# Scan runs' beginning: the second half's exponentials, logarithms and du moved behind the first units

## What is computed

```
xdbl = xm @ W_xp
dtr, Bm, Cm = jnp.split(xdbl, [DTR, DTR + DS], axis=-1)      # 64 + 16 + 16
dt = jax.nn.softplus(dtr @ W_dt + b_dt)
A = -jnp.exp(A_log)
def step(hst, inp):                                          # over 1024 positions
    dA = jnp.exp(dt_t[:, :, None] * A)
    hst = hst * dA + (dt_t * x_t)[:, :, None] * B_t[:, None, :]
    y = jnp.einsum('bds,bs->bd', hst, C_t)
```

## Time and profile before

| | |
|---|---|
| median of three executions | 1942.12 us (1942.08 to 1942.58) |
| the profiled execution | 1945.84 us |
| its span from first to last instruction | 1943.5 us |
| busy: TensorE, VectorE, ScalarE, GpSimd | 95%, 82%, 73%, 54% |
| mean granted TensorE clock | 0.975 |
| first scans of runs 0 to 5 | 208.2, 446.3, 669.9, 853.7, 1083.5, 1265.7 us |

### The profile page before, as it was taken

How to read it: one execution, slowest core, us unless ns; L and a number is a source line. 1 busy time by engine, 2 the same in 40 slices (tenths; PEclk the granted TensorE clock), 3 DMA queues, 4 the chain that set the end, 5 groups by cost and what they waited for, 6 DMA issues and landing times.

```text
span 1943.5 us, 32682 instructions
## 1 busy us (share of the span) xinstructions
PE 1845.3 (95%) x12312; PEld 1337.9 (69%) x12312; DVE 1600.7 (82%) x2125; ACT 1425.8 (73%) x2661; POOL 1048.6 (54%) x603
## 2 busy tenths in 40 slices
PE   6989899999999999999999999999998999999997
PEld 3664899948998599969995799689974333332323
DVE  5565899768998699989995999889987999999742
ACT  3426899468993899799974999799954377777775
POOL 3031599526994299939980699479944400003000
PEclk9989899998999999999999999999999799999999
DMA  5023111021111111101110121021101111111000
GB/s 202 1 85 99 59 57 55 32 72 43 56 59 37 51 54 60 51 24 55 56 44 2 40 60 56 24 72 58 58 15 32 38 42 38 37 37 36 17 23 22
DMA packets 57547, 95.18 MB, mean 49 GB/s; under 512 B 14951, under 2 KB 23559, under 8 KB 55982
## 3 DMA queue, kind: packets, MB, share of 16 engines
q1 hardware_dynamic: 55854, 88.90, 15.2%
q0 software_dynamic: 1536, 4.20, 0.7%
HBM read 73.55 MB, written 6.91 MB: 41 GB/s over the span
## 4 chain that ended last, share of the span: by engine, by line
PE 63%; POOL 14%; ACT 8%; DVE 8%; issue 6%; DMA 1%; SPq 1%; DVEq 0%; ACTq 0%; POOLq 0%
POOL A L1019 13%; PE PS L865 10%; PE PS L840 10%; PE PS L256 8%; PE PS L1603 6%; PE PS L1556 6%; PE PS L1763 5%; PE PS L846 5%; PE PS L265 3%; DVE A L1569 2%; PE PS L441 2%; PE PS L872 1%; ACT A L931 1%; ACT A L908 1%; PE PS L243 1%
## 5 line engine op out<-in xcount | busy, mean ns | idle before, releaser
L1019 POOL TENSOR_TENSOR A<-A 128x1024 f32<-128x1024 f32 x384 | 897.6, 2396 | 223.2 <-ACT small L923 111.0
L931 ACT ACTIVATE A<-A,negA 128x512 f32<-128x512 f32 x768 | 547.3, 715 | 34.0 <-DVE A L1000 24.4
L1000 DVE TENSOR_TENSOR_SCAN A<-A,PS 128x512 f32<-128x512 f32 x384 | 436.2, 1201 | 44.8 <-PE PS L846 23.8
L1000 DVE TENSOR_TENSOR_SCAN A<-A,small,PS 128x512 f32<-128x512 f32 x384 | 451.2, 1259 | 5.3 <-ACT A L931 5.3
L865 PE MATMUL PS<-ident,A 128*128 128x128 f32 x3072 | 408.5, 276 | 20.4 <-ACT A L737 13.3
L840 PE MATMUL PS<-A 128*128 128x128 f32 x3072 | 393.8, 276 | 0.9 <-ACT A L915 0.6
L865 PEld LDWEIGHTS PS<-ident,A 128*128 128x128 f32 x3072 | 352.3, 143 | 30.0 <-ACT A L737 15.9
L840 PEld LDWEIGHTS PS<-A 128*128 128x128 f32 x3072 | 368.1, 192 | 2.3 <-DVE A L1000 2.0
L1569 DVE TENSOR_REDUCE A<-PS 128x1 f32<-128x512 f32 x512 | 319.3, 681 | 38.9 <-PE PS L1556 37.3
L1800 ACT ACTIVATE A<-PS 128x512 f32<-128x512 f32 x512 | 267.2, 603 | 101.9 <-PE PS L1763 101.6
L908 ACT ACTIVATE A<-A,small 128x512 f32<-128x512 f32 x320 | 228.6, 714 | 17.3 <-PE PS L846 16.8
(11 more groups left out here) (194 smaller groups left out, 1842.7 us busy)
## 6 DMA issues: line engine op xcount, KB each, us to landing
A<-scrc SPq DMA_DIRECT2D x192, 256.0 KB, 3.1
A<-A SPq DMA_DIRECT2D x360, 32.0 KB
scr<-A SPq DMA_DIRECT2D x4, 1024.0 KB, 4.8
W<-in_wa SPq DMA_DIRECT2D x2, 1536.0 KB, 9.7
X<-in_x SPq DMA_DIRECT2D x4, 512.0 KB, 5.3
scr<-W SPq DMA_DIRECT2D x128, 1.5 KB
out<-X SPq DMA_DIRECT2D x4, 512.0 KB, 2.9
W<-in_w SPq DMA_DIRECT2D x1, 1984.0 KB, 7.3
```

Source lines behind the costliest of these rows:

```text
L931: e.activation(A_B[i % 4], r.DT[:, dt, ci * 512:(ci + 1) * 512], ACT.Exp, scale=negA[:, r.n, dt * 16 + s:dt * 16 + s + 1]).then_inc(*decay ...
L1000: e.tensor_tensor_scan(h, a, u, init, ALU.mult, ALU.add).then_inc(*scanned.up((q, i)))
L1019: e.tensor_tensor(h, h, CB[k % 2].unsqueeze(1).broadcast_to([128, 2, 512]), ALU.mult).then_inc(*weighed.up((q, pair)))
```

## The change

The first half of the sequence goes through its inputs alone. In `inputs_s` the exponentials and logarithms are cut in two (two channel groups d at a time, 1024 columns), and those of the second half move into `run_s`, behind the first diagonals and ahead of `more(3)`; VectorE's delta and du of the second half move into `run_v`, ahead of scan 4; the transposes of its du move in `run_t` behind `form_u(7)`, all four together; only |v| and max(v, 0) of the second half stay. `more(3)` moves on TensorE from behind du's transposes to behind `form_u(3)`. `PARTS` becomes 0, 2, 2, 4, and layer 1's fused product is cut into three: first half at `more(1)`, second at `more(2)`, bias at `more(3)`. VectorE, not ScalarE, copies the second half's x_dbl. ScalarE scales all four du tiles of the first half in every run, and copies two; VectorE copies the other two. `form_u(0)` to `form_u(3)` lie in banks of dt, not of du, and no longer wait for the copies; `form_u(4)` does. What VectorE does `meanwhile` (adding a gathered layer output to X, or X's moments) comes ahead of its first max(v, 0).

```diff
@@ project_dt_t
-            w.wait_ge(*act.at(("xd_twin", r.q, c)))
+            w.wait_ge(*(act if c == r.order[0] else dve).at(("xd_twin", r.q, c)))
@@ inputs_t
             more(1)
-            banks.seek(3)
+            banks.seek(4)
             project_dt_t(e, w, r, r.order[1])
...
             more(2)
-            banks.seek(4)
+            banks.seek(0)
             for j in range(4):
                 turn_du_t(e, w, r, 0, j)
-            more(3)
-            banks.seek(0)
@@ inputs_s
+        def decline_s(e, w, r, p, d):
+            g = DUD[:, p, 2 * d:2 * d + 2, :]
+            w.wait_ge(*act.at(("abs", r.q, 2 * d + 1, r.order[p])))
+            e.activation(g, g, ACT.Exp, scale=-1.0).then_inc(*act.up(("exp", r.q, p, d)))
+        def log_s(e, w, r, p, d):
+            g = DUD[:, p, 2 * d:2 * d + 2, :]
+            w.wait_ge(*act.at(("exp", r.q, p, d)))
+            e.activation(g, g, ACT.Ln, bias=1.0).then_inc(*act.up(("ln", r.q, p, d)))
...
-            size(0)
-            decline(0)
-            copy_xd_s(e, w, r, r.order[1])
-            log(0)
+            size(0, 0)
+            decline_s(e, w, r, 0, 0)
+            size(0, 1)
+            log_s(e, w, r, 0, 0)
+            decline_s(e, w, r, 0, 1)
+            log_s(e, w, r, 0, 1)
             more(1)
-            size(1)
+            size(1, 0)
+            size(1, 1)
...
-            decline(1)
-            log(1)
             more(2)
@@ first_state: third value, who scales and copies on VectorE
-            return r.G[j], Bt[:, 4 * r.order[0] + j, 0:1], r.q >= 2 and j >= 2
+            return r.G[j], Bt[:, 4 * r.order[0] + j, 0:1], j < 2
@@ copy_xd_v (new), delta_v (new)
+            w.wait_ge(*pe.at(("xd", r.q, c)))
+            e.tensor_copy(XD[0:96, c * 512:(c + 1) * 512], bank(("xd", r.q, c))[0:96, :]).then_inc(*dve.up(("xd", r.q, c)))
+            e.tensor_copy(XD2[64:128, c * 512:(c + 1) * 512], bank(("xd", r.q, c))[0:64, :]).then_inc(*dve.up(("xd_twin", r.q, c)))
...
+            w.wait_ge(*dve.at(("relu", r.q, 2 * d + 1, c)))
+            w.wait_ge(*act.at(("ln", r.q, p, d)))
+            e.tensor_tensor(t, t, g, ALU.add).then_inc(*dve.up(("delta", r.q, p, d)))
+            w.wait_ge(*dve.at(("delta", r.q, p, d)))
+            e.tensor_tensor(g, t, u, ALU.mult).then_inc(*dve.up(("du", r.q, p)))
@@ inputs_v
+            if meanwhile:
+                meanwhile()
+            relu_v(e, w, r, 0)
+            copy_xd_v(e, w, r, r.order[1])
+            for d in range(2):
+                delta_v(e, w, r, 0, d)
+            relu_v(e, w, r, 1)
@@ run_t
                     else:
-                        w.wait_ge(*first_copied(r, i))
+                        w.wait_ge(*act.at(("abs", q, i, r.order[1])))
+                        w.wait_ge(*dve.at(("relu", q, i, r.order[1])))
+                    if k == 1:
+                        first_half(w, r)
...
                 form_u(i + 3)
-                if 1 <= i < 5:
-                    turn_du_t(e, w, r, 1, i - 1)
+                if i == 0 and more:
+                    banks.seek(0)
+                    more(3)
+                if i == 4:
+                    banks.seek(0)
+                    for j in range(4):
+                        turn_du_t(e, w, r, 1, j)
@@ run_s
             for j in range(4):
-                if not first_state(r, j)[2]:
-                    scale_du_s(e, w, r, j)
+                scale_du_s(e, w, r, j)
...
                 spread_b(1, j)
+            for d in range(2):
+                decline_s(e, w, r, 1, d)
+                log_s(e, w, r, 1, d)
             more(3)
@@ run_v
+                if i == 4:
+                    if late:
+                        late()
+                    for d in range(2):
+                        delta_v(e, w, r, 1, d)
                 if i in (5, 6):
                     copy_du_v(e, w, r, 1, i - 5)
@@ layer 1: fuse_t(..., n, m) makes product m for m < 2 in bank 2 + m, the bias for m = 2; fuse_v is late()
-                inputs_t(e, w, r, ..., lambda part: fuse_t(e, w, b) if part == 2 else None)
-                run_t(e, w, r, lambda p: turn_back_t(e, w, r, p, y1))
+                inputs_t(e, w, r, ..., lambda part: fuse_t(e, w, b, part - 1) if part else None)
+                run_t(e, w, r, lambda p: turn_back_t(e, w, r, p, y1), None, lambda part: fuse_t(e, w, b, part - 1))
-                inputs_s(e, w, r, lambda part: None)
-                run_s(e, w, r, y1, lambda part: fuse_s(e, w, b))
+                inputs_s(e, w, r, lambda part: fuse_s(e, w, b) if part == 2 else None)
+                run_s(e, w, r, y1, lambda part: None)
@@ layer 2
-        GATES = [(m, c) for m in (2, 3, 0, 1) for c in range(2)]
+        GATES = [(m, c) for c in range(2) for m in (2, 3, 0, 1)]
-        PARTS = (slice(0, 0), slice(0, 1), slice(1, 4), slice(4, 8))
+        PARTS = (slice(0, 0), slice(0, 2), slice(2, 4), slice(4, 8))
-                w.wait_ge(*pe.at(("mx", b, m, c) if m >= 2 else ("mx", b, 1, 1)))
+                w.wait_ge(*pe.at(("mx", b, m if m >= 2 else 1, c)))
-                run_t(e, w, one, None, begin_two)
+                run_t(e, w, one, None, begin_two, lambda part: z_t(e, w, b, 1, z_jobs(1)[PARTS[part]]))
```

More of the change, by code:

```diff
@@ L756, in first_half, with relu_v, delta_v, inputs_v @@
                 w.wait_ge(*first_copied(r, j))
-        def inputs_v(e, w, r, meanwhile=None, late=None):
+        def relu_v(e, w, r, p):
+            c = r.order[p]
+            for m in range(4):
+                w.wait_ge(*act.at(("abs", r.q, m, c)))
+                e.tensor_scalar(r.DT[:, m, c * 512:(c + 1) * 512], bank(("dt", r.q, m, c)), col(r.bdt, m), 0.0, ALU.add, ALU.max).then_inc(*dve.up(("relu", r.q, m, c)))
+                banks.give(("dt", r.q, m, c), dve.now())
+        def delta_v(e, w, r, p, d):
+            c = r.order[p]
+            g, t, u = DUD[:, p, 2 * d:2 * d + 2, :], r.DT[:, 2 * d:2 * d + 2, c * 512:(c + 1) * 512], r.U[:, 2 * d:2 * d + 2, c * 512:(c + 1) * 512]
+            w.wait_ge(*dve.at(("relu", r.q, 2 * d + 1, c)))
[3 more added lines that the diff above has]
+            e.tensor_tensor(g, t, u, ALU.mult).then_inc(*dve.up(("du", r.q, p)))
+        def inputs_v(e, w, r, meanwhile=None):
             q = r.q
@@ L761, in inputs_v @@
                 e.tensor_scalar(diag[:, m, :], ident[:, :], col(r.dcol, m), None, ALU.mult).then_inc(*dve.up(("diag", q)))
-            for p, c in enumerate(r.order):
-                o = slice(c * 512, (c + 1) * 512)
-                for m in range(4):
-                    w.wait_ge(*act.at(("abs", q, m, c)))
-                    e.tensor_scalar(r.DT[:, m, o], bank(("dt", q, m, c)), col(r.bdt, m), 0.0, ALU.add, ALU.max).then_inc(*dve.up(("relu", q, c)))
-                    banks.give(("dt", q, m, c), dve.now())
-                if meanwhile and p == 0:
-                    meanwhile()
-                w.wait_ge(*dve.at(("relu", q, c)))
-                w.wait_ge(*act.at(("ln", q, p)))
-                e.tensor_tensor(r.DT[:, :, o], r.DT[:, :, o], DUD[:, p, :, :], ALU.add).then_inc(*dve.up(("delta", q, p)))
-                w.wait_ge(*dve.at(("delta", q, p)))
-                e.tensor_tensor(DUD[:, p, :, :], r.DT[:, :, o], r.U[:, :, o], ALU.mult).then_inc(*dve.up(("du", q, p)))
-            if late:
-                late()
-            for j in range(4):
-                if first_state(r, j)[2]:
-                    scale_du_v(e, w, r, j)
+            if meanwhile:
[5 more added lines that the diff above has]
+            relu_v(e, w, r, 1)
             for j in range(4):
@@ L789, in store_c_sp @@
         def store_c_sp(e, w, r):
-            w.wait_ge(*act.at(("xd", r.q, r.order[1])))
+            w.wait_ge(*act.at(("xd", r.q, r.order[0])))
+            w.wait_ge(*dve.at(("xd", r.q, r.order[1])))
             e.dma_start(scrc[r.q], XD[80:96, :]).then_inc(*transfer(f"c_store{r.q}").up(0))
@@ L820, in take_v, with run_t @@
                 e.tensor_copy(o, PS[:, j, :]).then_inc(*taken.up((r.q, p, j)))
-        def run_t(e, w, r, back=None, early=None):
+        def run_t(e, w, r, back=None, early=None, more=None):
             q = r.q
@@ L843, in form_u @@
                         for j in range(4):
-                            w.wait_ge(*(dve.at(("scaled", q, j)) if k == 0 and first_state(r, j)[2] else scaled.at((q, k, j))))
+                            w.wait_ge(*scaled.at((q, k, j)))
                         for j in range(4):
@@ L929, in decay @@
                     w.wait_ge(*scanned.at((q, i - 4)))
-                w.wait_ge(*dve.at(("delta", q, r.order.index(ci))))
+                w.wait_ge(*dve.at(("delta", q, r.order.index(ci), 1)))
                 e.activation(A_B[i % 4], r.DT[:, dt, ci * 512:(ci + 1) * 512], ACT.Exp, scale=negA[:, r.n, dt * 16 + s:dt * 16 + s + 1]).then_inc(*decayed.up((q, i)))
@@ L972, in program, with run_v @@
         TAKEN_AT = 71
-        def run_v(e, w, r, y, back=None):
+        def run_v(e, w, r, y, back=None, late=None):
             q = r.q
```

(7 more changed lines are left out.)

31 lines of the change are left out of this document (12 added, 19 removed).

## The result

The changed kernel takes **1987.12 us** (median of four, 1983.78 to 1988.57) against 1942.35 for the kernel before beside it (1942.08 to 1948.18): ratio 1.0215, 95% interval [1.0199, 1.0231]. It is slower, as forecast, but by 45 us and not by 30, outside the range of 1955 to 1981. Its profiled execution is 1987.85 us, the span 1986.1 (1943.5 before), and the mean granted TensorE clock 0.962 (0.975 before).

What follows compares the result with a forecast made beforehand. Each scan run was taken as a full pipe once started, so late beginnings arrive at its end. Order 18.3, clock 7.5, first add-up 2, runs 0 and 1 2: 29.8 us slower, 1972 us, range 1955 to 1981.

Steps and rivals of the forecast that it cites:

- steps 1 to 5: Beginnings of runs 2 to 5: first scan 4.0 us earlier in run 2, unit 4's decay later, 18.3 in all.
- the catch: Step 4, run 2: gate jobs moved behind unit 3 hold ScalarE's copies and loop, so unit 4's decay comes 4.7 us later.
- Half clock behind the new gap: TensorE after its new 3.9 us idle stretch, runs 2 to 5: 1.9 us lost a run, 7.5 for four.
- The later gap before the first add-up: TensorE's wait before the first add-up grows in runs 2 and 4 because ScalarE is later: 2 us in all.
- the part on the clock: TensorE's granted clock drops after idle stretches: 7.5 us in four runs, 2 for the first add-up, 2 in runs 0 and 1.
- the spare 1.94: Runs 0 and 1: scan 10 had waited 1.94 us for TensorE, which was to take up scan 4's delay of 1 to 1.5.
- worse: Rival: all new gaps cost 2.9, runs 0 and 1 lengthen by 2 to 3 more each; 42 us, 1984; chance 0.10.
- The rule that I left out of the sum: GpSimd beside VectorE's second-half delta and du slows them: up to 1.9 us more in each of runs 0 and 1.
- The clock holds: Rival: TensorE's new gap costs no clock; 18.3 + 2 = 20 us, 1962; chance 0.15.
- taken up: Rival: the late decay is caught up before GpSimd rules; no change, 1942; chance 0.05.
- everything stands ready: Rival: ScalarE never waits in a beginning; 13.8 us faster, 1928; chance 0.08.
- no more than some 5% to spare: Full pipe of a scan run: nothing in it has more slack, so a late start arrives at the run's end.

Runs made afterwards that it cites:

- e8_all_after: The changed kernel with the edits of e1_warm, e4_pool_waits and e7_copies_after together: 1952.28 us, ratio 1.0036 to the kernel before.
- v1_copies: The kernel before with ScalarE's two copies of the second half's du two units earlier (loop steps 7 and 8, not 9 and 10): 1931.74 us, ratio 0.9939.
- e7_copies_after: The changed kernel with ScalarE's two copies of the second half's du two units earlier: 1968.47 us, ratio 1.0116 to the kernel before.
- e1_warm: The changed kernel with 34 unread identity transposes on TensorE between du's transposes and unit 0, filling the new gap: 1967.71 us, ratio 1.0121 to the kernel before.
- e5_half_jobs: The changed kernel with one of two matmuls left out of each of the four moved gate jobs in runs 2 to 5: 1971.24 us, ratio 1.0141.
- e3_logs_back: The changed kernel with the second half's exponentials and logarithms back ahead of ScalarE's last gate copies: 1990.32 us, ratio 1.0239 to the kernel before.
- run 0: Not an experiment: the first of the kernel's six scan runs (0 to 5), in layer 1; 183.8 us in the kernel before, 187.4 in the changed one.
- e6_warm_pool: The changed kernel with the edits of e1_warm and e4_pool_waits together: 1967.31 us, ratio 1.0113 to the kernel before.
- v2_bias: The kernel before with layer 1's bias product moved to `more(1)`, in the wait for dt: 1940.51 us, ratio 0.9993.
- e4_pool_waits: The changed kernel with GpSimd's products waiting for VectorE's second-half du, and VectorE's work on X behind its x_dbl copies: 1973.88 us, ratio 1.0149.

## Why the prediction was wrong, step by step

**Runs 2 to 5 were right, in mechanism and size.** Three differences between run lengths separate the terms. The order (steps 1 to 5 with "the catch"): predicted 18.3, measured 18.3 (e8_all_after less v1_copies). Half clock behind the new gap: predicted 7.5, measured 7.4 (e7_copies_after less e8_all_after: 1.7, 2.4, 1.7, 1.6). The later gap before the first add-up: predicted 2, measured 2.9 (11.95 less 9.01). Sum 27.8 predicted, 28.6 measured. The three differences make up 28.6 by construction, so only each by itself is a test, and the agreement to a tenth is partly luck: e8_all_after has the moments of X in run 3 back in their old place (unit 4's decay 0.7 earlier than in e1_warm), and by e1_warm alone the half clock is 7.2 at unit 4's decay but 5.1 at the ends of the runs. The moves inside them are shown by e5_half_jobs (TensorE's moved jobs) and by e3_logs_back (what ScalarE does before its scalings).

**The step that failed is the last sentence of the part on the clock:** "Units 0 to 3 and the bias product at half clock in runs 0 and 1 go beyond the spare 1.94 by 1 each: 2." It measured 10.8, and these 8.8 us more decide: without them the median would be near 1978, inside the range. The mechanism named is the right one, and e1_warm shows that the clock, with what it brings about, is the whole loss: with the gap filled these two runs are 3.6 us shorter than before (0.96 and 0.95 of full clock over their beginnings, where the kernel before had 0.94 and 0.88), so that the lower clock costs 14.4. The size was wrong because I let the low level end as it does in runs 2 to 5, after some 6 us, and did not carry it on through the 32 products with two columns (3.63 to 6.83) and the units behind them. The kernel before could have warned me: there the clock falls behind this very product (the two rows of its run 0 above), although TensorE does not pause. The rival "worse" has exactly this sentence (bias product and units 4 to 7 at half clock too), and its 1984 came nearest; I gave it 0.10. Its sum was off, too: by its own terms it comes to 38 to 40, not 42, and so to 1980 to 1982. Of its "2 to 3 more each" run 0 shows 2.6 more than my 1, run 1 6.2.

**The rule that I left out of the sum applies in run 1, one step after the clock.** GpSimd was to meet only the last of the four operations at worst. It met the first two, for 3.8 us by the rows, because the bias product at half clock held VectorE back by 4.55 us while ScalarE went on and carried GpSimd's first states. That agrees with the Trainium skill (GPSIMD Engine Reference, section 1, Specifications), which names VectorE instructions with two SBUF inputs as those that contend; by the rows I had 1.9 us a run at most, one operation's worth. e6_warm_pool shows that this cost hangs on the clock and adds nothing once the clock holds.

**4.1 us lie in layer 3, which the change does not touch.** I had no term for it. It is not this change's alone: v1_copies, which is faster than the kernel before, has 3.4 us more behind run 5. Granted clocks of TensorE (the column after its busy time) in the first two 40 us behind the last product, in the kernel before, the changed kernel and v1_copies:

```profile
1424.20:1464.20 40.00, 37.81 (x155) 1.00 0.02 4
1464.20:1504.20 40.00, 31.20 (x111) 0.91 0.16 37
```

```profile
1462.80:1502.80 40.00, 37.82 (x149) 0.96 0.02 4
1502.80:1542.80 40.00, 31.19 (x107) 0.87 0.15 35
```

```profile
1404.60:1444.60 40.00, 37.81 (x150) 0.96 0.03 4
1444.60:1484.60 40.00, 31.20 (x108) 0.87 0.15 35
```

The engine's busy time in these two is the same to 0.01 us, only the clock differs, by 0.04 in each, and by 0.05 in the fourth such stretch (0.91 against 0.96); in the third it is 0.02 and 0.01 higher, in the others equal within 0.01. Behind run 5 the kernel before and v2_bias have 519.3 and 519.2 us, the other twelve kernels 521.5 to 523.5. That the clock is what makes it longer is read from these windows; which of two courses it takes, and why, was not tried and stays open. In the same way the 183 us before run 0, the same code in all, vary from 179.6 to 184.0.

**The rivals.** "The clock holds" is e1_warm, which had to be made; "taken up" and "everything stands ready" are refuted by run lengths (39.4 us longer in all, with unit 4's decays of runs 2 to 5 together 26.1 us later, and their ends 28.6: what is late there arrives, with something added). Nothing was caught up, as the full pipe of the earlier trace rows said; "no more than some 5% to spare" was too narrow a reading, since ScalarE is busy for 73.01 of the 80 us there, but TensorE and GpSimd have less.

## What to carry to other kernels

When work is moved so that a gap opens on TensorE, price the clock behind it by what stands there, and look up the longest stretch at the lower level in the nearest rows: here TensorE was back at full clock after 6 us in run 2, where 512-column matmuls follow, and stayed low for more than twice as long in run 0, where two-column products follow. No run put the one kind of work in the other's place. A gap that cannot be avoided can be filled: 34 idle transposes of 3.9 us gave back 19 us. Before a beginning is rebuilt, look for the copy that a full pipe waits for at its start: moving two copies by two units, one line of the kernel, gave 13 us (0.6%), and beat the rebuilt beginning by 2.8%.

## What the runs showed of the hardware

- The same 32 matmuls of two columns take 3.63 us at full clock and 6.83 at the lower one, and 16 transposes 1.91 and 3.65.
- In run 0 the granted clock was 0.50 in two stretches of 6 us and 0.65 in the next, after TensorE had been idle for 4.18 us, though it was busy all the time from 203.05 on. With two gaps of 2.56 and 1.76 us and 1.94 us of transposes between them (e4_pool_waits, run 1) it was still 0.98 over the bias product.
- Directly behind the 32 two-column matmuls the granted clock is low without any pause of TensorE: 0.54 and 0.60 over du's transposes in runs 0 and 1 of the kernel before, 0.60 over the matmuls of dt in v2_bias, 0.69 and 0.68 over units 4 to 7 in e1_warm (run 0) and e4_pool_waits (run 1), each time after 0.97 to 1.00 over the product itself. Where the product was moved (v2_bias), the low stretch moved with it. It is not certain: in run 0 of v1_copies, the same code as in the kernel before up to there, the clock stays 1.00. What in this product brings the fall about was not tried.
- A VectorE operation with two inputs in SBUF, 1024 columns wide, takes 1.22 us by itself and 2.98 to 3.27 when a GpSimd product of the same width, also in SBUF, is already under way. The one that comes second pays: in e7_copies_after, run 1, the GpSimd product that begins 0.35 us after such an operation leaves it at 1.22 and itself takes 3.09 instead of 2.36, and VectorE's next one, begun under it, takes 3.27 (GpSimd's times are rough).
- The stretch behind run 5, with nothing changed in it, took 519.2 and 519.3 us in two kernels and 521.5 to 523.5 in twelve (one profiled execution each), with other granted clocks in its first 160 us where they were compared.
